# A router front of four sequences moved from the start of an FFN stage into the attention stage before it

## What is computed

```
x = x + 0.5 * L0_ffn(norm(x))    # 8 experts, top-2 router
x = x +       L0_attn(norm(x))   # attention on cos/sin features
x = x + 0.5 * L0_ffn(norm(x))    # the same FFN again
x = x + 0.5 * L1_ffn(norm(x))    # 16 experts and a causal attention
x = x +       L1_attn(norm(x))   # selective scan
x = x + 0.5 * L1_ffn(norm(x))
```

```
# L0_attn: Q, K, V = x@W + b; theta = Q / wavelength + phase
sim = cos(tq) @ cos(tk).T + sin(tq) @ sin(tk).T
out = softmax(sim / sqrt(128)) @ V @ Wo.T + bo
# L0_ffn, on xf = norm(x) as (4096, 128)
logits = xf @ gate_w.T                  # 8 experts
w, sel = top_k(logits, 2); w = softmax(w)
out = sum_e w_full[:, e] * (xf @ expert_w[e].T)
```

## Time and profile before

| | |
|---|---|
| median of 3 runs | 1669.47 us (1667.58 to 1669.6) |
| the profiled execution | 1665.65 us |
| its span in the trace | 1663.5 us |
| mean granted clock of TensorE | 0.92 |
| PE, PEld busy | 84%, 62% |
| DVE, ACT, POOL busy | 70%, 31%, 32% |

### The profile page before, as it was taken

One profiled execution on the slowest core, in us unless ns is written; L12 is line 12 of the kernel. 1 busy time (PEld: TensorE's weight loads), 2 busy tenths in 40 slices (PEclk: granted clock), 3 DMA queues, 4 the chain that ended last, 5 costly groups with the idle time before them and its releaser, 6 DMA issues.

```text
span 1663.5 us, 21345 instructions
## 1 busy us (share of the span) xinstructions
PE 1404.0 (84%) x7226; PEld 1033.1 (62%) x7226; DVE 1172.5 (70%) x2629; ACT 513.2 (31%) x999; POOL 533.9 (32%) x447
## 2 busy tenths in 40 slices
PE   2887886595999999976888878878878599999998
PEld 2884545595899999952333333333323489999996
DVE  3786763585577776532998899999999557777753
ACT  2203444200222222223545445455353022222221
POOL 1150000001000000002788788888899100000000
PEclk9998997797899999986998989989998799999998
DMA  5550000553333333301332222323222233333330
GB/s 154 205 185 1 1 0 1 203 206 102 103 103 103 103 103 103 102 1 46 84 101 79 78 91 78 98 70 93 93 96 73 98 108 109 109 109 109 109 109 13
DMA packets 93162, 155.11 MB, mean 93 GB/s; under 512 B 11703, under 2 KB 21374, under 8 KB 92926
## 3 DMA queue, kind: packets, MB, share of 16 engines
q1 hardware_dynamic: 93054, 153.76, 28.5%
HBM read 150.31 MB, written 3.41 MB: 92 GB/s over the span
## 4 chain that ended last, share of the span: by engine, by line
PE 68%; DVE 16%; issue 8%; POOL 3%; ACT 2%; DMA 2%; DVEq 0%; POOLq 0%; SPq 0%; ACTq 0%
PE bank L1080 21%; PE bank L1198 7%; PE bank L1083 7%; PE bank L942 5%; PE bank L1142 3%; PE bank L973 2%; PE bank L1040 2%; DVE xe L1557 2%; DVE hs L1557 2%; DVE both L1549 2%; PE bank L1025 2%; POOL both L598 2%; PE bank L1092 2%; PE bank L1022 2%; PE bank L982 2%
## 5 line engine op out<-in xcount | busy, mean ns | idle before, releaser
L1080 PE MATMUL bank<-wqkv_sb,xe 128*128 128x192 f32 x2048 | 370.5, 334 | 10.0 <-DVE xe L1493 9.8
L1080 PEld LDWEIGHTS bank<-wqkv_sb,xe 128*128 128x128 f32 x2048 | 340.1, 194 | 21.4 <-DVE xe L1493 15.0
L1198 PE MATMUL bank<-both,ident 128*128 128x512 f32 x512 | 267.4, 650 | 17.3 <-DVE both L1549 16.4
L566 POOL TENSOR_TENSOR rstd<-ve,half_neg 128x4 f32<-128x4 f32 x32 | 37.6, 1173 | 734.0 <-DVE ve L1251 734.0
L843 ACT ACTIVATE bank<-dt,A 128x512 f32<-128x512 f32 x256 | 172.7, 685 | 169.6 <-DVE xe L1557 92.8
L1198 PEld LDWEIGHTS bank<-both,ident 128*128 128x128 f32 x512 | 105.0, 212 | 151.2 <-issue 108.3
L598 POOL TENSOR_TENSOR both<-du,prob 128x512 f32<-128x512 f32 x128 | 161.1, 1271 | 36.0 <-DVE xe L1557 19.8
L598 POOL TENSOR_TENSOR both<-du,prT 128x512 f32<-128x512 f32 x128 | 160.8, 1271 | 17.0 <-DVE hs L1557 12.5
L1557 DVE TENSOR_TENSOR_SCAN hs<-bank,both 128x512 f32<-128x512 f32 x128 | 153.7, 1212 | 0.0
L1557 DVE TENSOR_TENSOR_SCAN xe<-bank,both 128x512 f32<-128x512 f32 x128 | 152.8, 1210 | 0.3 <-issue 0.3
L942 PE MATMUL bank<-exp_sb,xe 128*128 128x128 f32 x1024 | 128.1, 283 | 27.1 <-DVE xe L1376 26.5
(11 more groups left out here) (261 smaller groups left out, 2011.4 us busy)
## 6 DMA issues: line engine op xcount, KB each, us to landing
dt<-w_rows SPq DMA_DIRECT2D x128, 256.0 KB, 4.2
du<-w_rows SPq DMA_DIRECT2D x128, 256.0 KB, 5.2
prob<-bc_dram SPq DMA_DIRECT2D x64, 256.0 KB, 3.3
prT<-bc_dram SPq DMA_DIRECT2D x64, 256.0 KB, 3.3
dt<-g_dram SPq DMA_DIRECT2D x32, 256.0 KB, 5.6
du<-g_dram SPq DMA_DIRECT2D x32, 256.0 KB, 6.7
g<-g_dram SPq DMA_DIRECT2D x32, 256.0 KB, 6.5
u<-g_dram SPq DMA_DIRECT2D x32, 256.0 KB, 6.4
```

Source lines behind the costliest of these rows:

```text
L566: pool.tensor_tensor(rstd[:], ve[:], half_neg[:, 0:NT], ALU.pow).then_inc(ln_rstd, 1)
L1080: m = pe.matmul(bank[4 + j // 2][:, (j % 2) * 3 * HD:(j % 2 + 1) * 3 * HD], x_e, wqkv_sb[:, e, :], start=(e == 0 and j % 2 == 0), stop=(e ...
L1198: pe.matmul(bank[4 + k % NH][:], ident[:], hc[k % HRING], start=False, stop=(SUM_RANK[k] == sums_of(k // UNITS, k % NH))).then_inc(hc_used, 1)
```

## The change

The front of group 0 of stage 2 is issued inside stage 1. DVE makes its statistics in `main(4)`, after the angle work for sequence 5 and before the division of sequence 4, and `gnmr` at the start of `main(7)`, the last sequence. POOL takes the power for it before that of sequence 6. PE and ACT issue one piece of the front after each score tile of `main(7)` (PE from the second tile on), and all three issue the rest after the last value products. The logits go to bank 4 in place of bank 1. `normed(s)` waits until the transposes of s - 1 are done, and for all angle parts of the attention. Stage 2 then starts with the expert products at once. Stage 0 is unchanged.

```diff
-def ffn_clock(front, front_at, *more):
+def ffn_clock(front, first, front_at, *more):
-    return [(front(G), HALF * (G - 1), front_at) for G in range(NB // GROUP)] + list(more)
+    return [(front(G), HALF * (G - 1), front_at) for G in range(first, NB // GROUP)] + list(more)
...
             def norms(layer):
                 for b in range(NB):
+                    if layer == 1 and b == NB - 2:
+                        group_rstd(1, 0)
                     rstd_of(layer * NB + b)
...
                 if layer in (0, 2):
-                    for G in range(NB // GROUP):
+                    for G in range(1 if layer == 2 else 0, NB // GROUP):
                         group_rstd(layer // 2, G)
...
-            def ffn(layer, r):
+            def ffn(layer, r, early=False):
...
                         act.wait_ge(gnmr_made, seen(2 * r + G + 1))
-                        act.wait_ge(xT_ps, seen(g - 1))
+                        act.wait_ge(xT_ps, seen(g if early else g - 1))
+                        if early:
+                            act.wait_ge(frac_made, seen(4 * NB))
...
+                group = ffn(2, 1, early=True)
+
                 def main(b, par, ahead):
                     act.wait_ge(acc_ps, seen(b))
                     for k in range(NT):
                         act.wait_ge(s_ps, seen(NT * b + k + 1))
                         act.activation(PT[:, k, :], bank[2 + k % 2][:], ACT.Exp, scale=1.0 / math.sqrt(P)).then_inc(p_made, 1)
                         step(ahead, k, (0,))
+                        if b == NB - 1:
+                            next(group)
                     finish(ahead)
 
                 overlapped(front, main)
+                finish(group)
...
                             k = NT * s + j
-                            m = pe.matmul(bank[1][:, k * E1:(k + 1) * E1], gxT[b][:, j * P:(j + 1) * P], gate_sb[:], start=True, stop=True)
+                            m = pe.matmul(bank[4 if early else 1][:, k * E1:(k + 1) * E1], gxT[b][:, j * P:(j + 1) * P], gate_sb[:], start=True, stop=True)
...
+                    if early:
+                        pe.wait_ge(turn_used, seen(2 * NB))
...
                         m.then_inc(s_ps, 1)
                         step(ahead, k, (0, 1))
+                        if b == NB - 1 and k:
+                            next(group)
...
                 def main(b, par, ahead):
                     for _ in range(3):
                         next(ahead, None)
+                    for _ in range({NB // 2: 5, NB - 1: 1}.get(b, 0)):
+                        next(group)
 
                     dve.wait_ge(acc_ps, seen(b + 1))
```

More of the change, by code:

```diff
@@ L694, in front @@
                     act.wait_ge(g_out, 16 * GROUP * (2 * r + G))
-                    act.activation(grows[:], bank[1][:, 0:P], ACT.Copy).then_inc(gT_sb, 1)
+                    act.activation(grows[:], bank[4 if early else 1][:, 0:P], ACT.Copy).then_inc(gT_sb, 1)
                     yield
+                if early:
+                    return front(0)
                 def prep():
@@ L709, in prep @@
                     yield
-                steps = ffn_clock(front, (6, 7, 8, 9, 10, 11, 17, 21), *([(prep(), HALF, (4, 10))] if layer == 0 else []))
+                steps = ffn_clock(front, 1 if layer == 2 else 0, (6, 7, 8, 9, 10, 11, 17, 21), *([(prep(), HALF, (4, 10))] if layer == 0 else []))
                 for u in FFN_CLOCK:
@@ L914, in front @@
                     pe.wait_ge(gw3_made, seen(2 * r + G + 1))
-                    pe.transpose(bank[1][:, 0:P], gwts[:].rearrange("p k e -> p (k e)"), ident[:]).then_inc(gT_ps, 1)
+                    pe.transpose(bank[4 if early else 1][:, 0:P], gwts[:].rearrange("p k e -> p (k e)"), ident[:]).then_inc(gT_ps, 1)
                     yield
+                if early:
+                    return front(0)
                 def prep():
@@ L944, in unit @@
                     m.then_inc(xe_used, 1)
-                steps = ffn_clock(front, (7, 8, 9, 10, 11, 12, 20), *([(prep(), HALF, (5, 9))] if layer == 0 else []))
+                steps = ffn_clock(front, 1 if layer == 2 else 0, (7, 8, 9, 10, 11, 12, 20), *([(prep(), HALF, (5, 9))] if layer == 0 else []))
                 for u in FFN_CLOCK:
@@ L1309, in front @@
                     dve.wait_ge(lg_ps, seen(r * NB + GROUP * (G + 1)))
-                    link(dve.tensor_copy(glg[:], bank[1][:, 0:GT * E1].rearrange("p (j e) -> p j e", e=E1)))
+                    link(dve.tensor_copy(glg[:], bank[4 if early else 1][:, 0:GT * E1].rearrange("p (j e) -> p j e", e=E1)))
                     link(dve.tensor_reduce(gm1[:], glg[:], AX, ALU.max))
@@ L1365, in residual @@
                     dve.scalar_tensor_tensor(seq(b), bank[7 - b % 2][:], 0.5, seq(b), ALU.mult, ALU.add).then_inc(acc_used, 1)
-                steps = ffn_clock(front, (0, 1, 2, 3, 4, 6, 13, 14, 15, 16, 19, 20), *([(prep(), HALF, (1, 2, 7, 13, 19))] if layer == 0 else []))
+                steps = ffn_clock(front, 1 if layer == 2 else 0, (0, 1, 2, 3, 4, 6, 13, 14, 15, 16, 19, 20), *([(prep(), HALF, (1, 2, 7, 13, 19))] if layer == 0 else []))
                 for u in FFN_CLOCK:
```

## The result

The changed kernel takes 1658.3 us (median of 10, 1655.09 to 1660.03) against 1668.82 for the one before (10 runs, 1661.35 to 1670.53): ratio 0.9937, 95% interval 0.9923 to 0.995, some 10.5 us faster. The forecast was 1662.3 (7.2 us faster than the 1669.47 of the first three runs), the range 1658.5 to 1667.2: the direction was right, and the time lies 0.2 us under the range. The profiled execution of the changed kernel took 1655.63, its span is 1653.5 us, 10.0 less than before.

The account below looks back on a forecast made before the run. Bound by an uncovered serial chain between attention and the first expert product, and in attention by a TensorE-VectorE loop. -14.2 + 3.6 + 2.1 + 1.3 = -7.2 us against 1669.47 gave 1662.3; range 1658.5 to 1667.2.

Parts of the forecast that it names:

- The gain: Front run beside attention's last sequence: logits ready at 276.15 instead of 290.42, 14.2 us saved.
- Cost 1: Statistics in main(4), ahead of sequence 4's division, delay the VectorE-TensorE loop without cover: 3.6 us.
- Cost 2: TensorE's clock falls after its longer idle stretch at sequence 6, 2.1 us, and again before sequence 7, 1.3 us.
- every us by which the row write comes earlier, measured against the end of attention, is a us of the kernel: Between attention and the first expert product: one uncovered serial chain, so an earlier row write shortens the kernel equally.
- Rival B: Clock costs less, nothing at sequence 7 and 0 to 1.3 at sequence 6: 1658.9 to 1660.2 us, chance 0.25.
- Rival C: Clock falls within the last sequence, slowing its fourth score tile and value products: 1665.9 to 1667.7 us, chance 0.29.
- Rivals D and E: Low clock from sequence 6 to the front's end, 1675.0; or normed(0) waits for the value products, 1666.8; 0.03 each.

Follow-up runs that it names:

- stats_in_wait: Changed kernel with VectorE's group statistics moved into its wait for the q product, main(4) and main(5), and POOL's power before sequence 7's: 1651.9 us, ratio 0.9903 to before.
- after_filled: Changed kernel plus overwritten 512-column products before the transposes from sequence 2 on, two each, six at sequence 6: 1651.0 us, ratio 0.9900 to before.
- stats_twice: Kernel before, with the 23 statistics operations made once more in main(4) where the change puts them, result unused: 1671.8 us, ratio 1.0021.
- fill_idle: Changed kernel plus four overwritten 512-column products in TensorE's idle stretch before sequence 6's transposes: 1656.3 us, ratio 0.9927 to before.
- behind_values: stats_in_wait, but TensorE and ScalarE issue the whole front behind the last score tiles and value products: 1658.0 us, ratio 0.9944 to before.
- after_delayed: Changed kernel plus 22 small VectorE copies between logits and top two, so the first expert product comes as late as before: 1664.7 us, ratio 0.9984.
- before_filled: Kernel before, plus two overwritten 512-column products before each group of transposes from sequence 2 on: 1665.2 us, ratio 0.9986.
- normed_first: stats_in_wait with gnmr one sequence earlier, in main(6), and normed(0) ahead of the first exp: 1651.0 us, ratio 0.9892 to the kernel before.

## Why the prediction came out as it did

**The gain** of 14.2 us was right: 14.4 at the first product where the statistics cost nothing (stats_in_wait), and from the first score tile to the row write within 0.2 us of the layout (25.9 against 26.1). Inside it the value products started 0.5 us earlier than laid out (12.7 us after the first tile against 13.2), because the waits for ScalarE were shorter.

**Cost 1**, 3.6 us: the period of sequence 5 to 6 became 20.47 us instead of 17.05, 3.4, shown alone by after_filled (20.46, at full clock) and by stats_twice (20.58). That the loop gives no cover was right.

**Cost 2**, 2.1 and 1.3 us: 2.5 and 1.3 (19.52 for the next period, and 250.46 to 255.35, 4.9, in the last). Both falls that the forecast counted took place, in all four profiles of the changed kernel. fill_idle, where both stay away, shows the price of the first. The prediction took the first as dearer because its idle stretch is longer; that reason isn't borne out, since behind_values had the same 2.5 and 1.3 us behind stretches of 3 us.

The sum, -7.2, stands at the row write as -7.0.

**The step that failed** is the first one, "every us by which the row write comes earlier, measured against the end of attention, is a us of the kernel", taken as if the rest of the program took as long in both programs. The sum held no term for it, neither a value nor a width: the rest is 1356.1 to 1364.4 us in the fifteen profiles of the experiments and the two first ones, at instructions that are the same from the first product on. Its part here was -3.0 us in the first pair of profiles, which with the -7.0 makes the 10.0 of their spans, and -4.4 in the means; after_delayed shows 2.7 by time (0.3 to 5.0) with the gain taken out. The place of these 3 us is shown, nearly all of them in the scan; their cause stays open. Smaller, and of the same kind: the profile of before was read as typical in attention, where it had one fall and two of the four profiles have two, 2.6 us later at the first product. Both widths belong in the range; with 3 us on the lower side it would have begun at 1655.5.

That the time fell 0.2 us outside the range and not inside is chance: the forecast was set against 1669.47, the median of three runs, and ten runs gave 1668.82, 0.65 less. The 3.3 us between -7.2 and -10.5 are not: the interval of the result is 8.3 to 12.9 us faster.

**Rival B**, 1658.9 to 1660.2, came nearest to the measured 1658.3, but for a reason that isn't there: the clock did cost its 3.8 us.

**Rival C** is refuted. The clock was 1.00 from 254 to 284, though transposes part the tiles. The Trainium skill ("TensorE: Matmul & The Clock Gate", Part 4: PE-mode transpose) says that the full clock doesn't engage for transposes. The traces agree where transposes and 8-column products stood alone (behind_values, 0.59 on average from 272 to 286, and the earlier trace rows), and they show no fall where score tiles lie between them. Rivals D and E did not occur.

## What to carry to other kernels

Where two engines take turns, put extra work for one of them into its own wait for the other, not in front of the operation that the other waits for: here the same 23 operations cost nothing in the one gap and 3.4 us in the other, and another 3.8 us by TensorE's clock. Small transposes and narrow products are worth spreading between wide ones, not only to hide their waits: behind them they ran at half clock here. And before a sum of 7 us is compared with a run of 1660, ask by how much the untouched rest differs between executions and between programs, from several profiles, and put that into the range.

## What the runs showed that was not expected

- TensorE's clock fell at one or two of the six idle stretches of 3 us in four profiles of the same kernel, at sequence 2 or at 2 and 3, and in behind_values at sequences 2, 4 and 5. Overwritten products in such stretches, which add work and save only clock, make the kernel faster by 2.3 us (before_filled, 0.02 to 0.25%). Added to normed_first, they bring the first product 2.6 us earlier; the two falls in its profile account for 2.9 (1.7 + 1.2). The medians differ by 5.2, and 2.4 of that are again in the rest.
- In the scan some sequences take 3 to 4 us longer than the others, none, one or two in an execution, in a program whose instructions do not change; a small cast on VectorE takes 0.23 us alone and up to 4.29 while POOL works through its products.
